# A decoder block on one core: first feed-forward tile moved a slot or two later, its statistics split over two steps

## The reference, cut to what matters

```python
x = x + attn(_layernorm(x), q_w, q_b, k_w, k_b, v_w, v_b, o_w, o_b)   # causal self-attention
x = x + xattn(_layernorm(x), ctx, ctx)       # causal cross-attention, q = layernorm(x), k = v = ctx, no weights
x = x + ffn(_layernorm(x), W_up, W_down, W_gate, W_expert)

def ffn(x):
    routing_weights, _ = top_k(x @ W_gate.T, 2)             # 8 logits per row
    shared = relu(x @ W_up.T) @ W_down.T
    rw = softmax(routing_weights)
    return shared + rw.sum(-1, keepdims=True) * (x @ W_expert)
```

## Time and profile before

| what | value |
|---|---|
| median of 3 runs | 708.54 us (708.42 to 709.91) |
| profiled execution | 706.88 us |
| its span, first to last instruction | 705.0 us |
| PE, weight load, DVE, ACT, POOL busy | 95%, 74%, 70%, 71%, 36% of the span |
| mean granted clock of TensorE | 0.997 of 2.4 GHz |

### The profile page before, as it was taken

The page is one execution under the profiler, slowest core; times in us unless marked ns, Lnnn a source line. Parts: engine busy times, 40 slices in busy tenths (PEclk is TensorE's granted clock), DMA queues, the critical chain, the costliest instruction groups (busy, mean ns, idle before and its releaser), DMA issues.

```text
span 705.0 us, 13884 instructions
## 1 busy us (share of the span) xinstructions
PE 672.6 (95%) x4488; PEld 520.1 (74%) x4488; DVE 494.4 (70%) x1730; ACT 501.6 (71%) x1450; POOL 257.1 (36%) x391
## 2 busy tenths in 40 slices
PE   6998999999999999999978988999999999999998
PEld 5776777777877777677756765777767887777786
DVE  6668766766766676767878779978867777764632
ACT  5778877777876778787898878877768876763110
POOL 4745645333555345751654432553202102000100
PEclk9999999999999999999999999999999999999999
DMA  9753533336433464354955776464435344320101
GB/s 315 193 151 75 141 70 91 77 93 184 117 71 91 127 196 98 88 123 124 268 140 144 195 215 144 120 166 104 113 98 156 100 105 106 69 96 1 59 1 60
DMA packets 52326, 86.12 MB, mean 122 GB/s; under 512 B 8608, under 2 KB 16800, under 8 KB 52256
## 3 DMA queue, kind: packets, MB, share of 16 engines
q1 hardware_dynamic: 52256, 85.25, 46.0%
HBM read 27.55 MB, written 7.34 MB: 49 GB/s over the span
## 4 chain that ended last, share of the span: by engine, by line
PE 80%; ACT 7%; DVE 6%; issue 2%; DMA 2%; POOL 2%; SPq 1%; ACTq 0%; POOLq 0%; DVEq 0%
PE t L514 15%; PE m L553 14%; PE m L554 14%; PE m L555 14%; PE pv L547 10%; PE s L500 8%; ACT probs L944 3%; DVE probs L716 2%; PE m L514 2%; ACT prob L953 2%; PE m L619 1%; DMA stack<-stage 1%; POOL probs L1057 1%; PE m L568 1%; DVE prob L726 1%
## 5 line engine op out<-in xcount | busy, mean ns | idle before, releaser
L716 DVE CUSTOM_DVE_ANT_0 probs<-s,mask 128x128 f32<-128x128 f32 (+3 forms) x512 | 246.5, 483 | 124.2 <-PE s L500 122.0
L944 ACT ACTIVATE probs<-probs,negmax 128x128 f32<-128x128 f32 (+3 forms) x512 | 284.7, 559 | 44.3 <-DVE negmax L716 43.6
L514 PE MATMUL t<-ident,probs 128*128 128x128 f32 x1116 | 198.0, 276 | 10.6 <-ACT prob L953 7.1
L500 PE MATMUL s<-stack 96*128 96x128 f32 (+3 forms) x512 | 196.5, 392 | 2.9 <-DMA stack<-stage 1.7
L1057 POOL TENSOR_SCALAR probs<-probs,rsum 128x128 f32<-128x128 f32 (+3 forms) x256 | 133.4, 539 | 176.4 <-DVE rsum L730 176.0
L953 ACT ACTIVATE prob<-t 128x384 f32<-128x384 f32 (+1 forms) x225 | 121.5, 541 | 87.1 <-PE t L514 85.5
L514 PEld LDWEIGHTS t<-ident,probs 128*128 128x128 f32 x1116 | 140.5, 141 | 57.4 <-ACT prob L953 11.0
L500 PEld LDWEIGHTS s<-stack 96*128 96x128 f32 x512 | 97.4, 190 | 14.1 <-DMA stack<-stage 2.4
L944 ACT ACTIVATION_READ_ACCUMULATOR probs<-probs,negmax 128x1 f32 x512 | 99.1, 194 | 0.0
L726 DVE COPY prob<-t 128x256 f32<-128x256 f32 (+1 forms) x215 | 76.3, 355 | 29.8 <-PE t L514 29.1
L553 PE MATMUL m<-xT_hi,w_lo 128*128 128x512 f32 x192 | 78.4, 409 | 1.2 <-DVE xT_lo L784 1.2
(11 more groups left out here) (144 smaller groups left out, 956.6 us busy)
## 6 DMA issues: line engine op xcount, KB each, us to landing
stack<-stage SPq DMA_DIRECT2D x384, 128.0 KB, 2.3
xt<-in_x SPq DMA_DIRECT2D x16, 256.0 KB, 4.2
xres<-in_x SPq DMA_DIRECT2D x4, 1024.0 KB, 6.0
kraw<-in_ctxT SPq DMA_DIRECT2D x16, 256.0 KB, 3.0
cv<-in_ctx SPq DMA_DIRECT2D x16, 256.0 KB, 3.3
x<-xres SPq DMA_DIRECT2D x3, 1024.0 KB, 5.8
res<-x SPq DMA_DIRECT2D x8, 256.0 KB, 6.3
out<-res SPq DMA_DIRECT2D x2, 1024.0 KB, 4.7
```

The lines of the kernel that those rows point to most:

```text
L500: nc.tensor.matmul(score_tile(P, i), stack[0:RS, P % 2, h, 0, chunk(qb)], stack[0:RS, P % 2, h, 1, 0:N], start=True, stop=True).then_inc(s ...
L514: mm = nc.tensor.transpose(dst[:, chunk(qb - kb)], probs[:, (2 * P + h) % 3, OFF[qb] + PART * kb:OFF[qb] + PART * kb + PART], ident[:, :])
L716: nc.vector.tensor_tensor_reduce(probs[:, (2 * P + h) % 3, OFF[qb]:OFF[qb + 1]], score_tile(P, i), mask[:, T - N:T], -SCALE, BIG, ALU.add, ...
L944: nc.scalar.activation(tile, tile, ACT.Exp, bias=negmax[:, P % 2, h, qb:qb + 1], scale=-1.0, accum_out=total).then_inc(p_exp, 1)
```

## The change

All of it is placement. No instruction is added or removed.

- The transposes `FL` of the sequences 0, 1 and 2 start one slot later (43.0 becomes 43.1, and so on in threes). Their gate starts two slots later (44.2 becomes 44.4).
- The up tiles of sequences 0 and 1 stood five slots apart; they now start at +0, +5, +9, +14 from the first, which is itself two slots later, so that the expert tiles stay where they were. For sequence 2 up, expert and down all go two slots later. For sequence 3 nothing moves.
- The last down tile of sequences 0 and 1 goes one slot later (51.5 becomes 51.6).
- The statistics for `f` = 0 go from 41.1, 41.2, 41.4, 41.5 to 41.4, 41.6, 42.0, 42.0, the last two beside the value matmuls of step 42. Its normalizations go from 42.0, 42.0, 42.1, 42.1 to 42.4, 42.5, 42.6, 42.6. `f_scale(0)` on POOL moves from the end of step 41 to the head of step 42, ahead of the wait for the normalizations.
- For the queries of sequence 2 the first statistics go from 43.1 to 43.2 and the normalizations from 44.1, 44.4, 44.4, 44.5 to 44.3, 44.4, 44.5, 44.6.
- Following from the plan: turned blocks use an `m` bank at 42.5 and 42.6 more than before, and no longer at 45.4, 46.1, 46.6 and 47.3 (nor at the same places of steps 53 to 55).

```diff
 def turns_at(f):
-    u = feed_start(f)
+    u = feed_start(f) + 1
     return [u + 3 * m for m in range(KC)]

 def gate_at(f):
-    return feed_start(f) + (8 if f == B - 1 else 10)
+    return feed_start(f) + (8 if f == B - 1 else 12)

 def up_at(f, m):
-    return gate_at(f) + 4 + (4 if f >= B - 2 else 5) * m
+    return gate_at(f) + 4 + 4 * m + (0 if f >= B - 2 else (m + 1) // 2)

 def down_at(f, m):
     if f >= B - 2:
         return expert_at(f, KC) + 4 * m
-    return expert_at(f, KC) + 5 * m if m < 2 else feed_start(f + 1) + 5 * (m - 2)
+    return expert_at(f, KC) + 5 * m if m < 2 else feed_start(f + 1) + 6 * (m - 2)

 def stats_slots(j):
     if j == B + 2:
-        return [z + 25, z + 28, z + 29, z + 31]
+        return [z + 26, z + 28, z + 29, z + 31]

 def norm_slots(j):
     if j == B + 2:
-        return [z + 33, z + 36, z + 36, z + 37]
+        return [z + 35, z + 36, z + 37, z + 38]

 def f_stats_slots(f):
     z = PAIRS * (PAIRS * (f + B + 1) + 1)
-    return [z + 1, z + 2, z + 4, z + 5]
+    return [z + 4, z + 6, z + 8, z + 8] if f == 0 else [z + 1, z + 2, z + 4, z + 5]

 def f_norm_slots(f):
     z = PAIRS * (PAIRS * (f + B + 1) + 2)
-    return [z, z, z + 1, z + 1]
+    return [z + 4, z + 5, z + 6, z + 6] if f == 0 else [z, z, z + 1, z + 1]

 # GpSimd, per step
                     for qb in range(NT):
                         scaled(s, 1, qb)
+                if s == f_stats_slots(0)[-1] // PAIRS:
+                    f_scale(0)
                 for j in range(B + 1, 2 * B):
...
-                for f in range(B):
+                for f in range(1, B):
                     if s == f_stats_slots(f)[-1] // PAIRS:
                         f_scale(f)
```

## The result

The change makes the kernel slower: 711.14 us (median of 21 executions, 708.34 to 714.26) against 708.38 us for the kernel before (21, 705.51 to 711.59), a ratio of 1.0042 with a 95% interval of 1.003 to 1.0054. The forecast was 707.3 us, and its range ended at 709.4.

A forecast was written before the change was run, and what follows sets the result against it. PE, busy 95% of the span, was taken as the bound, so only its waits or lower clock could yield gains. Terms -0.25 + 0.7 - 0.2 - 1.5 = -1.25 us took 708.54 to 707.3 us, range 705.2 to 709.4.

The forecast's parts named there:

- Part 1: Statistics of sequence 0: values of step 42 start earlier, limited by the stack landing; -0.25 us, bounds 0 and -0.9.
- Part 2: Normalizations in 42.4 to 42.6: DVE falls behind and the values of step 44 wait for a turned copy; +0.7 us.
- Part 3: Gate of sequence 0: its wait for xT_hi shrinks with one more slot; -0.2 us, bounds -0.6 and +0.3.
- Part 4: Handovers from sequence 0 to 1 and 1 to 2: bank waits go, smaller new ones appear; -0.75 us each, -1.5 together.
- Part 5: The rest: closer up tiles, turned blocks alternating between two banks, moved quarter tiles and the tail; nothing.
- The slower one: DVE enters step 44 about 1.25 us late and cannot recover, so PE waits repeatedly; +1.8 us, 710.3 us, chance 0.14.
- The clock stays up: Values of step 42 avoid the lower clock, gaining 1.65 us more; -2.9 us in all, 705.6 us, chance 0.2.

The follow-up runs named there:

- r0: The kernel before, unchanged, profiled once more: 706.42 us in one execution at clock 1.000.
- r1: The changed kernel, unedited, profiled once more: 710.57 us in one execution at clock 0.997.
- e1: Kernel before with only the change's statistics and normalizations moves (sequence 0, f_scale, queries of sequence 2): 709.54 us, ratio 1.0021.
- e3: Changed kernel with the four normalizations of sequence 0 early, at 42.1, 42.1, 42.2, 42.2: 709.92 us, ratio 1.0029 to the kernel before.
- e8: Kernel before with only the four normalizations of sequence 0 moved, to 42.4, 42.5, 42.6, 42.6: 709.25 us, ratio 1.0011.
- e2: Kernel before with only the change's tile moves (transposes, gate, up, last down tile): 710.12 us, ratio 1.003.
- e6: Kernel before with the change's tile moves for sequences 1 and 2 and the last down tiles, sequence 0 otherwise as before: 707.79 us, ratio 0.9992.
- e5: Kernel before with, for sequences 1 and 2, transposes four slots apart and a later gate; last down tile one slot later: 707.95 us, ratio 0.998.
- e9: e5 with the last transposes of sequences 1 and 2 one slot earlier: 705.23 us, ratio 0.9964 to the kernel before.
- e4: e2 with the last down tile of sequences 0 and 1 back at its old place: 709.54 us, ratio 1.0024 to the kernel before.
- e10: e9 with the gate of sequences 1 and 2 one slot earlier: 707.45 us, ratio 0.9984 to the kernel before.

## Why the prediction was wrong

The steps that failed are terms of the sum. The late normalizations were put at +0.7 us and cost 1.69; the later tiles of sequence 0 were put at -0.2 us, with nothing for the steps behind them, and cost 0.96 and 0.39; the two handovers were put at -1.5 us and gave -0.27 together, since the gate's bank comes free later than the forecast had it; and steps 54 and 55, put at nothing, cost 0.39.

**Part 1, the mechanism right, the number luck.** The values of step 42 start at 424.76 (forecast 424.71) behind a `stack` wait in one piece. But that start follows the landing, which differs by 0.7 us between two executions of the kernel before: in the second pair the values start at 425.38 (r0) and 425.52 (r1), and no gain shows. The statistics beside the values had slack only because those values ran at 1.2 GHz, as they did in the trace that was read: DVE then idles 1.52 us. In e1 and e3, at 2.4 GHz, DVE is still in them when the values end. What that costs PE is not shown: in e1 PE waits for DVE nowhere between the values and `FL(0, 0)`, and in e3 its wait stands behind the early normalizations as well.

**Part 2, the term that was mis-sized.** Forecast +0.7 us, bounds 0 and 1.4; measured +1.69 (e1 against r0). Three things were left out. The first consumer, `FL(0, 0)`, was never compared with the new time of its last normalization, and waits for it: 0.95 us in the changed kernel, 2.21 in e1 and in e8. DVE then waits for PE in turn, so the two lose time one after the other. And `query_lo` was said to stay in time because ACT set the start of the values of step 44; DVE set it, 0.5 us later than before. Only the wait inside the values was foreseen (0.6 us; it is 0.77). (Of the turned blocks of 42.5 and 42.6 only the second is new in an `m` bank; the plan before has 42.5 in one too.)

**Part 3, wrong in sign.** Forecast -0.2 us; measured +0.96 in steps 44 and 45 (e2; e6, without the edit, is back at 19.97 us). The wait of the gate did go. But this window has DVE busy 19.3 of 20 us, and taking a quarter tile of PE work out of it only brings PE sooner to turned blocks whose copy DVE has not made: 0.72 us at 455.00 (454.50 in e2). The prediction priced PE's waits at this place one by one and did not ask which engine is the bound once PE has less to do.

**Part 4, one term wrong.** Forecast -0.75 us for each handover; measured +0.03 and -0.30. `FL(1, 0)` and the down tile lost their waits and `FL(1, 1)` and `FL(1, 2)` got those named (0.92 and 0.17 us). The failed term is the gate, put at -0.18: it waits 1.12 and 0.71 us for the down tile's bank. That bank is emptied later than one would think from a move of one slot. In the kernel before, PE's values of step 52 and then DVE:

```profile
524.24 2.36 PE L547 MATMUL pv<-prob,cv 128*32 128x512 f32 x32
...
527.34 0.42 DVE L716 CUSTOM_DVE_ANT_0 probs<-s,mask 128x256 f32<-128x256 f32 x1 [1.80 <-PE s L500]
...
527.69 0.69 DVE L834 TENSOR_TENSOR xt<-m,xt 128x512 f32<-128x512 f32 x1
```

In the changed kernel, where the values start at 525.63:

```profile
528.73 0.42 DVE L716 CUSTOM_DVE_ANT_0 probs<-s,mask 128x256 f32<-128x256 f32 x1 [2.39 <-PE s L500]
...
529.08 0.69 DVE L802 TENSOR_TENSOR xT_lo<-m,xT_hi 128x512 fp32r<-128x512 f32 x1
...
529.84 0.91 DVE L771 TENSOR_SCALAR V<-xres,mv,rstd 128x512 f32<-128x512 f32 x2
...
531.48 0.68 DVE L834 TENSOR_TENSOR xt<-m,xt 128x512 f32<-128x512 f32 x1
```

In both, DVE is released by the score tile 3.10 us after the start of the values. Before, the emptying (L834) came right behind that mask, 3.45 us after the start. Now it stands one slot further back in DVE's own order, behind an `xT_lo`, two normalizations, a mask and a copy: 5.85 us. The last quarter of the tile did move from ahead of the values to behind them, but it ends near 529.4, 2.1 us before DVE takes the bank, so the value matmuls are not what sets the time. The gate's first quarter, two slots later than before, finds only a few short score tiles and turned blocks on PE to pass the time. At the second handover it is 3.45 us before and 5.44 after. e5 and e9 show that the idea itself pays (up to 2.28 us) when the users of each bank stand further apart.

**Part 5, not nothing.** Steps 46 and 47 and steps 54 and 55 each lose 0.39 us. Turned blocks then alternate between two banks, and one of them waits 0.17 us as shown (about 0.32 by the distance of starts):

```profile
475.84 0.66 PE L514 MATMUL t<-ident,probs 128*128 128x128 f32 x4 [0.17 <-DVE prob L726]
```

The missing `m` banks are not enough for this. e9 has the same banks for the turned blocks of steps 54 and 55 as the changed kernel and one quarter more of PE work than it, and loses nothing there (20.76 us with two quarters more than before: 20.76 - 1.40 = 19.36 against 19.35). Where the up tiles leave PE a slot without a quarter must count too; that was not separated.

**The rivals.** The slower one had the right mechanism at the right place: DVE enters step 44 late and the turned copies cost PE. It was priced with that lateness carried through step 45 for good (710.3 us) and given 0.14. What the runs show in its place does not last beyond step 47, but the moved tiles add to it. "The clock stays up" did not happen in this execution nor in r1. The difference of the two kernels is the same 3.1 us at a mean clock of 1.000 and of 0.993, so the clock does not explain it.

**What stays open.** How the +0.96 us of sequence 0's tiles divides among transposes, gate and up tiles was not separated. How much the moved statistics add to the late normalizations is not fixed either, since e8's excess contains a longer stretch at the lower clock. Nor is it shown why the two halves of the change lose more in steps 44 and 45 together than one by one.

## What to carry to other kernels

When a producer is moved later, look first at its own first consumer, then at the work behind it. Moving tiles of the busiest engine out of a stretch gained nothing here, where a second engine is as full; ask who is the bound without them. With few buffers used in rotation, a delay of one user shifts a wait to the next one (e4), and more room at every use makes the waits smaller (e9). When a tile moves by one slot, look where its emptying lands in the queue of the engine that empties it: here one slot of DVE's work was 2.4 us.

## What the chip showed besides

- **Where the stretch at 1.2 GHz falls is mostly fixed; whether it comes is not.** In eight of the thirteen traces (the kernel before, the changed one, e2, e5, e6, e8, e10, r1) the clock is low at the values of step 42, and the window of steps 42 and 43 has a mean clock of 0.85 to 0.93. In r0, e1, e3, e4 and e9 it is 1.00. The same program did both: the values of step 42 took 4.01 us in one execution of the kernel before and 2.70 us in another (r0). e1 and e3 have a low stretch elsewhere, and e5 and e6 a second one. At the values of step 42 it cost 1.3 us in the kernel before (17.74 against 16.42 us for steps 42 and 43), and about 2.5 where it was longer (e5 and e10: 18.58 and 18.68 us against 16.12 in e9; the three are the same program up to there). The Trainium skill, "TensorE: Matmul & The Clock Gate", section "HAM oscillation — how this bites in real kernels", says that a wait for a transfer can send TensorE back to the lower clock. Here the length of the wait for `stack` just ahead does not tell the two apart: 0.32 to 2.50 us in the eight, 1.01 to 2.29 us in the five.
- **Much of the spread goes with the mean clock of an execution.** Over 87 executions of the kernel before the median is 706.15 us at 1.000 (13), 708.78 at 0.995 (33) and 710.17 at 0.993 (13). A change of 0.2% is read far better between executions of equal clock.
- **A landing under full queues is uncertain by 1 us or more.** The last loads of pair 43 came at 424.41 us in one execution of the kernel before and at 425.13 in another. Over the nine traces whose program is the same up to step 41, they came 14.3 to 15.7 us after the start of the values of step 40, with the transfers' share at 0.78 to 1.09 in the last 3 us before the values of step 42, and this alone moves the start of that step.
